# Moving one VectorE comparison ahead of two subtractions in a three-layer expert-attention kernel

## The reference

```python
x = x + 0.5 * _L0_ffn_ref(_layernorm(x), Wq, Wk, Wv, Ws, Wd, Wo)
x = x + _L0_attn_ref(_layernorm(x), ...)
x = x + 0.5 * _L0_ffn_ref(_layernorm(x), Wq, Wk, Wv, Ws, Wd, Wo)
```

```python
gate_v = jnp.einsum('btc,hec->bthe', x, Ws)
w, sel = jax.lax.top_k(gate_v, K)            # K = 2 of E = 8
wsig = jax.nn.sigmoid(w)
mix_v = jnp.einsum('bthk,bthke->bthe', wsig, one_hot(sel))
v = jnp.einsum('bthe,bted->bhtd', mix_v, proj_v)
probs = softmax((q * scale) @ k)             # 16 heads, 256 x 256 each
attn = probs @ v
gate_o = jnp.einsum('btc,hec->bthe', x, Wd)  # top 2 again, used as a mask
```

## Time and profile before

| | |
|---|---|
| median of 3 runs | 2602.04 us (2600.72 to 2605.43) |
| the profiled execution's own time | 2600.72 us |
| its span in the trace | 2597.4 us |
| PE busy | 2520.3 us (97%) |
| PE weight loads busy | 2300.8 us (89%) |
| DVE busy | 2126.9 us (82%) |
| ACT busy | 1938.1 us (75%) |
| POOL busy | 1140.0 us (44%) |
| mean granted clock of TensorE | 0.995 |

### The profile page before, as it was taken

How to read it: one execution, slowest core, us unless ns; L and a number is a source line. 1 busy time by engine, 2 the same in 40 slices (tenths; PEclk the granted TensorE clock), 3 DMA queues, 4 the chain that set the end, 5 groups by cost and what they waited for, 6 DMA issues and landing times.

```text
span 2597.4 us, 111277 instructions
## 1 busy us (share of the span) xinstructions
PE 2520.3 (97%) x45824; PEld 2300.8 (89%) x45824; DVE 2126.9 (82%) x3498; ACT 1938.1 (75%) x6117; POOL 1140.0 (44%) x1126
## 2 busy tenths in 40 slices
PE   3999999999999999999999999999999999999997
PEld 3898999989889899999898999999999998998997
DVE  5788888888888888888888888888888888887874
ACT  3777777777777777777777777777777777777775
POOL 2353544434435345344345344444444453444431
PEclk8999999999999999999999999999999999999999
DMA  4555555555555555655655655556556556555563
GB/s 128 148 152 142 142 154 144 154 148 155 148 151 147 152 150 155 157 149 149 153 159 144 154 154 154 153 146 164 145 150 156 149 152 152 150 144 151 153 160 98
DMA packets 519347, 387.55 MB, mean 149 GB/s; under 512 B 214080, under 2 KB 436160, under 8 KB 510656
## 3 DMA queue, kind: packets, MB, share of 16 engines
q1 hardware_dynamic: 518416, 379.60, 55.2%
q10 hardware_dynamic: 432, 0.85, 0.1%
HBM read 191.64 MB, written 188.74 MB: 146 GB/s over the span
## 4 chain that ended last, share of the span: by engine, by line
PE 79%; DVE 10%; ACT 7%; issue 3%; POOL 1%; DMA 1%; SPq 0%; DVEq 0%; ACTq 0%; POOLq 0%
PE psT L424 17%; PE psT L462 15%; PE psS L381 14%; PE psT L441 6%; PE psT L394 5%; DVE QK L668 5%; PE psT L443 5%; PE psT L442 5%; PE psT L436 5%; ACT PB L732 4%; PE psT L408 3%; ACT QK L741 2%; DVE NMAX L611 2%; DVE S L688 1%; PE psT L466 1%
## 5 line engine op out<-in xcount | busy, mean ns | idle before, releaser
L732 ACT ACTIVATE PB<-psS,NMAX 128x256 f32<-128x256 f32 x2048 | 948.9, 487 | 513.8 <-DVE NMAX L611 510.6
L611 DVE TENSOR_REDUCE NMAX<-psS 128x4 f32<-128x1024 f32 x512 | 602.8, 1219 | 27.0 <-PE psS L381 26.2
L462 PE MATMUL psT<-ident,PB 128*128 128x128 f32 x4096 | 549.2, 279 | 12.2 <-DVE QK L668 5.8
L424 PE MATMUL psT<-V,PT 128*64 128x64 f32 x16384 | 539.7, 224 | 14.2 <-issue 13.6
L424 PEld LDWEIGHTS psT<-V,PT 128*64 128x64 f32 x16384 | 501.4, 138 | 42.5 <-issue 17.4
L462 PEld LDWEIGHTS psT<-ident,PB 128*128 128x128 f32 x4096 | 444.3, 141 | 96.9 <-DVE QK L668 60.0
L668 DVE TENSOR_TENSOR QK<-psT,QK 128x512 fp32r<-128x512 f32 x512 | 340.6, 687 | 171.4 <-ACT QK L741 169.8
L732 ACT ACTIVATION_READ_ACCUMULATOR PB<-psS,NMAX 128x1 f32 x2048 | 450.2, 220 | 0.0
L381 PE MATMUL psS<-QK 64*128 64x256 f32 x6144 | 433.6, 287 | 0.0
L381 PEld LDWEIGHTS psS<-QK 64*128 64x128 f32 x6144 | 381.2, 186 | 42.9 <-issue 33.6
L828 ACT ACTIVATE PT<-psT 128x512 f32<-128x512 f32 x768 | 412.9, 618 | 7.9 <-PE psT L462 7.6
(11 more groups left out here) (116 smaller groups left out, 4266.3 us busy)
## 6 DMA issues: line engine op xcount, KB each, us to landing
Vd<-VM SPq DMA_DIRECT2D x128, 512.0 KB, 3.7
V<-Vd SPq DMA_DIRECT2D x128, 512.0 KB, 5.3
AOd<-AO SPq DMA_DIRECT2D x256, 256.0 KB, 3.6
PJd<-PJ SPq DMA_DIRECT2D x64, 512.0 KB, 2.6
PR<-PJd SPq DMA_DIRECT2D x64, 512.0 KB, 4.0
MIXd<-MIX SPq DMA_DIRECT2D x64, 128.0 KB, 1.8
MT<-MIXd SPq DMA_DIRECT2D x64, 128.0 KB, 4.7
MASKd<-MASKR SPq DMA_DIRECT2D x64, 128.0 KB, 3.6
```

Source lines behind the costliest of these rows:

```text
L424: last = eng.matmul(M[64 * u:64 * u + 64, (t * NT + it) * DH:(t * NT + it + 1) * DH], PT[:, t, jt, cols], V[:, pm % 2, 4 * r + t, jt, :], ...
L462: last = eng.transpose(M[:, jt * T + it * P:jt * T + (it + 1) * P], PB[:, ab, j, it, jt * P:(jt + 1) * P], ident[:, :])
L611: eng.tensor_reduce(NMAX[:, ab, :, :], psS[:, ab, :, :, :], AX_X, ALU.max, negate=True).then_inc(s_max)
L732: eng.activation(PB[:, ab, j, it, :], psS[:, ab, j, it, :], ACT.Exp, bias=NMAX[:, ab, j, it:it + 1], accum_out=SUM[:, p % 2, it, 4 * r + t ...
```

## The change

`equal(1, ...)` of quarter r = 2 is moved, on VectorE, from behind the two QK subtractions to ahead of them. Operation, operands and the value that it waits for are the same; nothing is added or removed.

```diff
@@ -661,13 +661,13 @@
                     dst = XT[:, (p + 3) % 4]
                     eng.wait_ge(s_xhi, p + 4)
                     eng.tensor_tensor(dst[:, 1, :], bank("xturn", p + 3)[:, 0:T], dst[:, 0, :].bitcast(F32), ALU.subtract).then_inc(freed("xturn", p + 3))
+                if r == 2 and runs(q):
+                    equal(1, GM[:, :, :], at + 7)
                 if works(n + 1):
                     for ab in range(2):
                         m = 2 * n + 2 + ab
                         eng.wait_ge(s_qhi, m + 1)
                         eng.tensor_tensor(QK[:, 1, ab], bank("qk", m).rearrange("p (k t) -> p k t", k=2), QK[:, 0, ab].bitcast(F32), ALU.subtract).then_inc(freed("qk", m))
-                if r == 2 and runs(q):
-                    equal(1, GM[:, :, :], at + 7)
                 if r == 0 and runs(q):
                     equal(0, GS[:, :, :], at + 1)
                 if r == 1 and runs(q):
```

## The result

| | before | changed |
|---|---|---|
| median, us | 2603.73 (2600.72 to 2605.55, 4 runs) | 2627.09 (2624.49 to 2635.09, 4 runs) |
| the profiled execution's own time | 2600.72 | 2628.41 |
| span in the trace | 2597.4 | 2626.3 |

The ratio is 1.0096, with a 95% interval of 1.007 to 1.0121. The kernel got slower by 23 us at the median, inside the range and on the forecast side; the forecast itself, 2638, was 11 us too high.

What follows compares the result with a forecast made beforehand. PE, busy for 97% of the span, was taken as the bound, so VectorE counts only where PE waits for it. Losses of 31.5 + 5.0 = 36.5 us in r = 2 gave 2638 us, range 2622 to 2650.

Steps and rivals of the forecast that it cites:

- That the edit's place is on the path: TensorE's transposes (line 462) wait for the QK subtractions (line 668), 60.0 us in total; this goes to near 97.
- That BT holds up EQ, and for how long: In r = 2, EQ waits until GpSimd's BT ends, taking about 1.97 us with AAN alone, 2.3 with both normalisations.
- the tail behind BT: In r = 2, EQ's time after BT's end: 0.55 us from one warm-up row, bounded by 0 and 0.72.
- rival (a): In r = 2, EQ is not blocked and the gap hides it: 2601 to 2602 us; chance 0.05.
- The sum for r = 2: Loss of 1.21 us in 26 passes with AAN alone and 0.83 in 6 with both normalisations: 36.5 us.
- What comes behind, costed at 0: After r = 2's QK pair, the fourth transpose's copy can start 0.2 us earlier, but nobody gains: 0 us.
- rival (b): EQ is blocked, but shifted transfers change line 688 in r = 0: 11 us either way, 2627 or 2649; chance 0.10.
- a sign of being wrong: The prediction is wrong if quarters r = 3 or r = 0 change length by more than a few tenths.
- AXN passes at 0: In r = 2 of 26 passes with AXN alone, BT is over and EQ fits the idle gap: loss 0.
- (c) the clock: TensorE's granted clock falls to 1.2 GHz from longer idling in 32 quarters: 54 us more, 2692; chance 0.02.
- (d) the order: In r = 2, BT comes second and waits for EQ instead: price near 0, chance 0.01.

Runs made afterwards that it cites:

- The reduce: Kernel before with an added one-input tensor_reduce of GM ahead of the QK pair in r = 2, EQ staying behind: 2604.88 us, ratio 1.0005.
- the moved BT: Changed kernel with the second half of BT ahead of the AAN normalisation on GpSimd: 2601.55 us, ratio 0.9993.

## Why the prediction was right, and which term was off

*That the edit's place is on the path.* Right. The weight loads' wait for the pair rose from 60.0 to 100.6 us, where 97 was said.

*That BT holds up EQ, and for how long.* Right, and the step most at risk, since it stood on one warm-up row; the 61 instances of line 675 in the same trace would have secured it. Predicted 1.97 and 2.30 us; 1.96 and 2.25 in the rows above; the tail behind BT 0.55 predicted, 0.56 measured. The reduce and the moved BT show the cause. The prediction let the tail go down to 0, and the rows don't support that: the 128 x 128 operation of line 688 ended 0.15 us after BT in all 18 instances that it held up, alone it takes 0.28, and EQ's 0.55 stands beside 0.68. In both the tail is the operation's own time less 0.13 us. "SBUF — State Buffer" of the Trainium skill, section "Who interferes with whom", says just this of an operation with two SBUF inputs, and that a tensor_reduce never contends on trn2; both agree with the 1.96 and the 0.68 us. It makes no exception for small GpSimd operations, and there the F that ran 0.69 us beside line 836 doesn't agree. The note in "Advanced Engine Details and Errata", section "VectorE Performance Modes", read as the whole rule, would have given rival (a).

*The sum for r = 2.* 31.5 + 5.0 = 36.5 us predicted, 30.1 + 4.3 = 34.4 measured. A quarter with AAN alone got 1.16 us longer at the median where 1.21 was said, one with both 0.78 us for 0.83.

*What comes behind, costed at 0.* VectorE's side was right: the copy starts with the transposes' end, and the row maxima follow the scores as before. But I followed only semaphore waits from there, and wrote under rival (b) that the transfers keep their place relative to r = 3. They don't all: the V load is issued in r = 2, before the hold-up, so it moved 1.2 us away from the next scores. This is the term that was mis-sized: 0 in the sum, 10.7 us measured back. The prediction itself had named quarters r = 3 that change by more than a few tenths as a sign of being wrong, and eight of these changed by 0.8 to 2.0 us. Rival (b) had the right kind of effect (transfers shifted against engines, 11 us, 2627) and the wrong spot: line 688's quarters r = 0 and r = 1 changed by 1.8 us in sum, and the give-back was in r = 3.

*The number.* That 10.7 us is so near the forecast's error of 11 is in part chance. Between the traces r = 2 cost 2.1 us less than the sum, while other quarters, warm-up and tail added 5.2 us for which the sum had nothing; and of the 27.7 us between the profiled executions the medians show 23.4. That the range held 2627 is luck in part too: its lower end came from a tail of 0 behind BT, and the tail was as forecast.

*AXN passes at 0, (c) the clock, (d) the order.* The AXN quarters moved by 0.1 us in sum. The granted clock of the changed kernel was 0.997 of 2.4 GHz on average, with the holes of the AAN quarters (1.10 us in the row above), so (c) was out. GpSimd was not the one to wait.

## What to carry to other kernels

Before moving a VectorE operation into an idle gap, look at what GpSimd does in the same microseconds and count the operation's SBUF inputs: with two it waited out the 128 x 1024 operations of GpSimd that had begun, BT and MB (1.96 us for 0.68), with one (0.68), or one of two from PSUM (0.69), it didn't. To see whether a kernel has this already, look for lines whose durations have two levels: here line 675 (0.68 and 1.6 to 2.4 us) and line 688 (0.28 and 1.9 to 2.5). Whether freeing line 675 from MB would gain anything was not run. A gap on one engine's timeline is not free time for every operation. And when a stage gets longer, look for holes without a releaser in the stages behind it: part of the loss may come back there. Here a later transfer gained as much as the edit had cost, and by two effects, of which the holes were the smaller one.

## What the runs showed of the hardware that I had not expected

TensorE stopped for 0.8 to 1.7 us in the middle of a run of products with no semaphore to wait for, in eight of the 26 quarters r = 3 with AAN alone in the profiled execution of before, each time until 1.3 to 1.5 us after a 16 KB instruction packet had landed. Issuing one 512 KB load 6.6 us later (839.86 where the scores of r = 3 began at 835.16, against 838.96 and 840.87) removed them from these quarters and made eight in r = 0; the product line's idle time fell from 14.2 to 5.0 us.

The packets themselves came late. The packet ahead of each of the eight holes, followed by its number in the queue, starts 1.5 to 2.3 us after the scores of its quarter in the kernel before. In the changed kernel seven of the same eight packets start 0.4 to 1.6 us after the scores, and with V's load later 0.3 us ahead of them to 1.3 us after; the eighth (842.8 in the kernel before) starts over 2 us ahead of the scores in both. That they queued behind the load's data fits all the runs. But no trace shows when a packet was asked for, so this much is inferred.
